# Fused Flamingo layers on one core: the 16-head attention's query projection in split operands, and POOL making all split parts in the layer-1 attention

## The reference

```python
q = (hidden_states @ Wq).reshape(B, Sq, H, D)
k = (encoder_hidden_states @ Wk).reshape(B, Skv, H, D)
v = (encoder_hidden_states @ Wv).reshape(B, Skv, H, D)
q = rmsnorm(q, gq)
k = rmsnorm(k, gk)
scores = jnp.einsum('bqhd,bkhd->bhqk', q, k) * scale
attn = jax.nn.softmax(scores, axis=-1)
out = jnp.einsum('bhqk,bkhd->bqhd', attn, v)
return out.reshape(B, Sq, H * D) @ Wo
```

## Time and profile before

| what | value |
|---|---|
| three runs | 3634.16, 3641.05, 3655.15 us (median 3641.05) |
| the profiled execution's own time | 3635.72 us |
| its span in the trace | 3633.9 us |
| mean granted PE clock | 0.944 of full speed |
| `l0_ffn` | about 245 to 458 us of the span |
| `l1_xattn` | about 458 to 1112 us, main part from about 641 |
| `l2_xattn` | about 1502 to 2920 us |

### The profile page before, as it was taken

The page is one execution under the profiler, slowest core; times in us unless marked ns, Lnnn a source line. Parts: engine busy times, 40 slices in busy tenths (PEclk is TensorE's granted clock), DMA queues, the critical chain, the costliest instruction groups (busy, mean ns, idle before and its releaser), DMA issues. The chain is left out here.

```text
span 3633.9 us, 43465 instructions
## 1 busy us (share of the span) xinstructions
PE 3207.4 (88%) x14597; PEld 1930.8 (53%) x14628; DVE 2598.7 (72%) x3488; ACT 1806.3 (50%) x3413; POOL 1401.9 (39%) x956
## 2 busy tenths in 40 slices
PE   6868888999996888799999999999999878997995
PEld 2337644333333555455555555555555456785763
DVE  6864679877765888377777877777777755665786
ACT  4644333666663445355555556556655332664220
POOL 1121178000000000166666667766666634223540
PEclk9978999999998999899999999999999888998998
DMA  3026736222218100244544454445454345665311
GB/s 127 37 110 228 265 120 164 59 57 58 62 29 175 29 1 1 82 163 152 176 151 158 161 165 167 157 152 167 154 165 136 104 190 200 239 250 189 139 70 58
DMA packets 229735, 478.69 MB, mean 132 GB/s; under 512 B 36224, under 2 KB 69632, under 8 KB 213649
## 3 DMA queue, kind: packets, MB, share of 16 engines
q1 hardware_dynamic: 223280, 459.19, 39.2%
q0 software_dynamic: 6240, 16.81, 1.3%
HBM read 387.51 MB, written 92.06 MB: 132 GB/s over the span
## 5 line engine op out<-in xcount | busy, mean ns | idle before, releaser
L2341 POOL TENSOR_TENSOR l2x_inflow<-l2x_dtu,l2x_rows_b 128x512 f32<-128x512 f32 x256 | 432.3, 1689 | 332.7 <-DVE l2x_state L2230 311.0
L178 POOL TENSOR_TENSOR ln_work<-ln_work,minus_half 128x4 f32<-128x4 f32 (+1 forms) x34 | 33.3, 978 | 1055.4 <-DVE ln_work L166 1055.3
L2230 DVE TENSOR_TENSOR_SCAN l2x_state<-l2x_decay,l2x_inflow 128x512 f32<-128x512 f32 x256 | 384.6, 1502 | 17.0 <-ACT l2x_decay L2104 17.0
L1300 DVE TENSOR_REDUCE l1x_mx<-psum 128x2 f32<-128x1024 f32 x256 | 308.2, 1219 | 96.0 <-PE psum L1142 94.5
L2044 ACT ACTIVATE l2x_probs<-psum,l2x_soft,l2x_norms 128x512 f32<-128x512 f32 x256 | 195.7, 775 | 321.3 <-DVE l2x_soft L2168 321.3
L2357 POOL TENSOR_TENSOR l2x_y_sum<-l2x_y_sum,l2x_state 128x512 f32<-128x512 f32 x224 | 340.6, 1521 | 33.0 <-DVE l2x_state L2239 33.0
L1257 ACT ACTIVATE l1x_split<-psum 128x1024 f32<-128x1024 f32 x256 | 262.2, 1025 | 154.5 <-PE psum L1142 154.5
L126 PE MATMUL psum<-l2x_probs_t,l2x_v_tok 128*128 128x512 f32 x512 | 238.5, 609 | 32.0 <-ACT l2x_probs_t L212 26.0
L2239 DVE TENSOR_TENSOR l2x_state<-l2x_state,l2x_rows_c 128x512 f32<-128x512 f32 x256 | 251.8, 984 | 6.7 <-issue 0.3
L126 PE MATMUL psum<-l2x_xt,l2x_wq 128*128 128x512 f32 x512 | 230.9, 595 | 7.8 <-issue 6.3
L126 PE MATMUL psum<-l2x_kt,l2x_qt 128*128 128x512 f32 x512 | 231.3, 595 | 4.0 <-ACT l2x_probs L2044 4.0
(11 more groups left out here) (446 smaller groups left out, 7311.6 us busy)
## 6 DMA issues: line engine op xcount, KB each, us to landing
l2x_rows_b<-l3x_xd_dram SPq DMA_DIRECT2D x256, 256.0 KB, 3.6
l2x_rows_c<-l3x_xd_dram SPq DMA_DIRECT2D x256, 256.0 KB, 3.5
l2w_raw<-l_w SPq DMA_DIRECT2D x38, 1024.0 KB, 6.3
l2x_wkv<-l2x_kv_dram SPq DMA_DIRECT2D x32, 1024.0 KB, 7.0
l2w_raw<-l_w SPq DMA_DIRECT2D x38, 512.0 KB, 4.6
l1x_heads_dram<-l1x_stage SPq DMA_DIRECT2D x32, 512.0 KB, 3.3
l2x_wq<-l_wq SPq DMA_DIRECT2D x16, 1024.0 KB, 7.2
l2x_wo<-l_wo SPq DMA_DIRECT2D x16, 1024.0 KB, 5.4
```

The source lines that it names most:

```text
L1300: main.drain(dve.tensor_reduce(mx[:, gg % 2, :, j, t], g["psum"][:, b:b + 2, :], AX.X, ALU.max), f"m{n}_0", banks=2)
L2230: dve.tensor_tensor_scan(state[:, s % KEPT, :], decay[:, s % 3, :], inflow[:, s % 3, :], 0.0, ALU.mult, ALU.add).then_inc(scan_done, 1)
L2341: pool.tensor_tensor(inflow[:, s % 3, :], dtu[:], rows_b[:, s % 3, :], ALU.mult).then_inc(inflow_ready, 1)
```

## The change

1. `l0_ffn` no longer makes split parts: the 12 loads, 12 ACT roundings, 12 POOL subtractions and 12 stores go.
2. `l1_xattn` makes them in its main part, with `SPLITS` = 20 pieces: the same 12 and 8 more of two heads of `l2_wq` each. SP loads, and stores 1 MB, in the loop over groups; POOL does both steps (a multiplication by one into float32r, and the subtraction). They use `stage`, for which SP first waits until all heads have been stored.
3. `l2_xattn` projects queries by `split_product` from `q_dram`. The weight is streamed by head, 512 KB each, two buffers. `xt` has two parts: ACT rounds all four chunks, DVE subtracts.
4. To make room: `k_sq` goes (the keys' squares are written into `q_sq`), `KEPT` is 6, `y_sum` has one buffer, so POOL's first addition of a unit waits for DVE's `skip_term` of the unit before.

```diff
@@ l0_ffn
-            def split_load(p):
...
-            def split_store(p):
...
-            def split_round(p):
...
-                act.activation(s_parts[:, 0], s_raw[:, p % 2], ACT.Copy).then_inc(s_hi, 1)
...
             for i in range(NB):
                 if i == 2:
                     scales()
-                split_rest(3 * i)
-                split_rest(3 * i + 1)
                 ln.pool(pool, i)
-                split_rest(3 * i + 2)
@@ l1_xattn, SP
+            def split_load(p):
+                k, b = divmod(p, 4)
+                if p >= SPLITS:
+                    return
+                if p < 12:
+                    src = a[("ctx_t", "l2_wk", "l2_wv")[k]].rearrange("(c p) n -> p c n", p=P)[:, :, b * S:(b + 1) * S]
+                else:
+                    src = a["l2_wq"][2 * (p - 12):2 * (p - 11)].rearrange("h p n -> p h n")
+                if p >= 2:
+                    sp.wait_ge(s_lo, p - 1)
+                sp.dma_start(s_raw[:, p % 2].rearrange("p (c n) -> p c n", c=2), src).then_inc(s_in[p % 2], 16)
+
+            def split_store(p):
...
+                sp.wait_ge(s_lo, p + 1)
...
+            for m in range(2):
+                for k in range(2):
+                    sp.wait_ge(staged_out[m][k], TILES // 2 * 16)
             for gg in range(GROUPS):
                 load_rows(gg)
                 if gg >= 1 and gg + SETS - 1 < GROUPS:
                     load_set(gg + SETS - 1)
+                if gg == 0:
+                    split_load(0)
+                if gg >= 1:
+                    split_store(gg - 1)
+                split_load(gg + 1)
+            sp.wait_ge(s_stored, SPLITS * 16)
@@ l1_xattn, POOL, behind the additions of the bias
+            one = g["ones"][:, 0:1].to_broadcast([P, 2 * S])
+            for p in range(SPLITS):
+                pool.wait_ge(s_in[p % 2], (p // 2 + 1) * 16)
+                if p:
+                    pool.wait_ge(s_stored, p * 16)
+                pool.tensor_tensor(s_parts[:, 0].bitcast(F32R), s_raw[:, p % 2], one, ALU.mult).then_inc(s_hi, 1)
+                pool.wait_ge(s_hi, p + 1)
+                pool.tensor_tensor(s_parts[:, 1].bitcast(F32R), s_raw[:, p % 2], s_parts[:, 0], ALU.subtract
+                                   ).then_inc(s_lo, 1)
             ln.pool(pool, NB - 1)
@@ l2_xattn
-KEPT = 8
+KEPT = 6
...
-            jobs += [(f"xt{(u + 1) // G2}_{c}", "act" if c % 2 else "dve") for c in range(DC)]
+            jobs += [(f"xt{(u + 1) // G2}_{c}", "dve") for c in range(DC)]
...
+            def query_weight(u, h):
+                if u < NU:
+                    if u or h >= 2:
+                        ring.wait_filled(sp, 0, f"q{u}_{h - 2}" if h >= 2 else f"q{u - 1}_{h + 2}")
+                    sp.dma_start(wq[:, h % 2].rearrange("p r c n -> p (r c n)").bitcast(F32),
+                                 g["q_dram"][u % G2 * 4 + h].rearrange("p r n -> p (r n)")).then_inc(wq_in[h % 2], 16)
...
-            weight(wq, "l2_wq", 0, wq_in)
+            query_weight(0, 0)
+            query_weight(0, 1)
...
             weight(wo, "l2_wo", 0, wo_in, rows=True)
-            ring.wait_filled(sp, 0, "q0_3")
-            weight(wq, "l2_wq", 1, wq_in)
+            for h in (2, 3):
+                query_weight(0, h)
+            for h in (0, 1):
+                query_weight(1, h)
...
-                    if n == 15 and u + 2 < NU:
-                        ring.wait_filled(sp, 0, f"q{u + 1}_3")
-                        weight(wq, "l2_wq", u + 2, wq_in)
+                    if n in (7, 8) and u + 1 < NU:
+                        query_weight(u + 1, n - 5)
+                    if n in (11, 13) and u + 2 < NU:
+                        query_weight(u + 2, (n - 11) // 2)
...
-                    ring.fill(product(pe, bank(f"q{u}_{h}"), [(wq[:, c, h * P:(h + 1) * P], xt[:, c, :])
-                                                              for c in range(DC)]))
+                    ring.fill(split_product(pe, bank(f"q{u}_{h}"), [
+                        ([wq[:, h % 2, k, c, :] for k in range(2)], [xt[:, k, c, :] for k in range(2)])
+                        for c in range(DC)]))
...
-                    for c in (1, 3):
+                    if u:
+                        ring.wait_filled(act, 0, f"q{u - 1}_3")
+                    for c in range(DC):
                         job = f"xt{u // G2}_{c}"
                         ring.wait_filled(act, 0, job)
-                        copy(act, "act", ring, job, xt[:, c, :], bank(job))
+                        act.activation(xt[:, 0, c, :], bank(job), ACT.Copy).then_inc(x_hi, 1)
...
+                        dve.wait_ge(x_hi, u // G2 * DC + c + 1)
+                        ring.drain(dve.tensor_tensor(xt[:, 1, c, :], bank(job), xt[:, 0, c, :].bitcast(F32),
+                                                     ALU.subtract), job)
...
                 if n == 1:
-                    since(pool, y_read, u - 1)
+                    since(pool, y_read, u)
```

More of the change, by code:

```diff
@@ L1015, in l1_xattn @@
         staged_out = [[sem(f"staged_out_{n}{k}") for k in range(2)] for n in "qk"]
+        s_hi, s_lo, s_stored = sem("s_hi"), sem("s_lo"), sem("s_stored")
+        s_in = [sem(f"s_in{k}") for k in range(2)]
         set_in = [sem(f"set_in{k}") for k in range(SETS)]
@@ L1371 @@
 GROUPS = NB * NG
+SPLITS = 20
 N_MAX = GROUPS * PAIRS * ST
@@ L1834, in l2_xattn @@
         b_in, c_in = [[sem(f"{n}_in{k}") for k in range(3)] for n in "bc"]
+        wq_in = [sem(f"wq_in{k}") for k in range(2)]
         ln = LayerNorm(g, sem)
@@ L2064, in context @@
                 if u < NU:
+                    if n == "k" and u:
+                        ring.wait_filled(act, 0, f"ssq{u - 1}")
                     for t in range(ST):
```

75 lines of the change are left out of this document (28 added, 47 removed).

## The result

The changed kernel took 3664.55 us (median of eight executions, 3639.33 to 3685.21) against 3641.16 us for the kernel before on the same chip: a ratio of 1.0071, 95% interval 1.005 to 1.0092. That is slower by 23 us, just over what a measurement can tell, and just outside the predicted range. The profiled execution is the slowest of the eight, 3685.21 us, 49.5 us above the profiled one of before.

| stage | before, us | after, us | difference | forecast |
|---|---|---|---|---|
| `l0_ffn` | 196.5 | 192.6 | -3.9 | -5 |
| layer-1 attention | 644.2 | 696.3 | +52.1 | +8 |
| 16-head attention | 1403.7 | 1401.0 | -2.7 | -14.5 |

What follows compares the result with a forecast made beforehand. PE, busy 88% of the span, was taken as the bound. The terms -14.5 (16-head attention), -5 (`l0_ffn`) and +8 (layer-1 attention) made -11.5 us: 3624 us for a profiled execution, 3630 for a median, range 3600 to 3662.

Steps and rivals of the forecast that it cites:

- stall = (4.1 - 3.4)/2 = 0.35: Layer-1 attention, SP's queue: maxima land 4.1 us after issue against 3.4 in reserve; +8 us, bounds 0 and 44.
- The clock rival: 16-head attention: slow PE clock after value 0's longer wait costs 1.7 us in each of 15 units; 3655 us, chance 0.12.
- the three signs of being wrong: Layer-1 waits over 1 us; value 0's wait unchanged at 1.65 us with units 2.6 us shorter; half clock after that wait.
- The rival of SP's queue: Layer-1 attention: the maxima's rows wait behind 1.5 MB at the slow rate, costing 44 us; 3666 us, chance 0.14.
- The reason given for the queue: Layer-1 attention: maxima issued on SP's queue behind a piece's store and load land late, as small transfers do not overtake.
- the bound of 2 us: Layer-1 attention: POOL's pieces blocking DVE's tiny instructions at a group's end; nothing expected, at most +2 us a group.
- the 96 us that one could fear: Layer-1 attention: DVE locked out by POOL's 40 instructions of 2.4 us, by the shared port rule alone; not expected.
- went as forecast: `l0_ffn`: without POOL's subtractions DVE is 2.1 us earlier in the last two batches; -5 us, bounds 0 and -8.
- A unit is shorter by 1.3 us, as forecast: 16-head attention: only queries 2 and 3 give their saving, 1.30 us a unit, -19.5 us over 15 units.
- the copies of `xt`: 16-head attention: ACT makes four copies instead of two, 1.0 us more in each of three batches; +3 us.
- The start: Start of the 16-head attention: the third weight comes 3 to 4 us late, against 2.6 us saved; +2 us (0 to 5).
- No other rival: Remaining rivals, 16-head attention: all of the PE gain arrives, 3602 us, chance 0.23; new product no faster, 3649 us, 0.03.

Runs made afterwards that it cites:

- pool_only: The changed kernel with POOL's splitting work in 16 groups without its loads and stores, only four pieces made with their DMAs (other output); 3620.20 us, ratio 0.9958.
- spaced_decay: The changed kernel with pieces' stores and loads in 18 groups only, and ACT's decays of steps 5 and 6 behind head 0's turned probabilities; 3677.21 us, ratio 1.0134.
- four_pieces: The changed kernel with 4 pieces of splitting instead of 20 in the layer-1 attention (other output); 3637.46 us, ratio 0.9982 to the kernel before.
- dma_only: The changed kernel with all 20 loads and stores of the pieces, but POOL working only on the last four (other output); 3674.32 us, ratio 1.0101.
- pool_wait: The changed kernel with POOL beginning each piece only when the next group's maxima are turned; 3688.37 us, ratio 1.0134 to the kernel before.

## Why the prediction was wrong

**The layer-1 attention is the step that failed**, in the size of one term: "stall = (4.1 - 3.4)/2 = 0.35, taken as 0.4 us in 20 groups, +8 us". The place was right, and so was why PE waits: the maxima land 2.2 to 5.9 us after their issue, and PE waits for their rows. Even the sum of the waits was near, 7.5 us in the first profile (5.5 for rows, the rest behind DVE), 10 and 14 in the other two. What failed is the price and the shape. They are not 0.4 us in twenty groups but 1.3 to 2.2 us in four to eight. And I priced a wait at its own length. The clock rival had the price of a half clock, but I put it into the 16-head attention alone, at 1.7 us a time; in the layer-1 attention show groups of 12.26 us at whole clock, and I never asked what a wait would do there. The term measured +52 us in the first profile, and 44 of them are half clock. Two of the three signs of being wrong that I had named came: waits of over 1 us for the rows, and half clock behind value 0's wait. The rival of SP's queue came out at 3666 us, near the 3664.55 measured, by a sum of waits (44 us) that no profile shows. Its number was right by luck.

**The reason given for the queue was half right.** The Trainium skill's rule (DMA: Bandwidth & Descriptors, "Queues, rings and completion order") that descriptors of one ring are consumed in ring order fits the landing of 5.9 us at 785.03. But with the pieces on another queue, where the maxima were held up less often, the rows of some groups were later still, 6.62 us of wait. So large transfers in flight can hold up a small one of another queue as well. That run also changed when the pieces go out and which engine issues them, so it does not price the two reasons.

**The engines of this layer.** "Only the three tiny instructions at a group's end can be blocked; a piece would have to run there": one did, piece 0, and the bound of 2 us was its price (1.96 against 0.17 us, and a wait of 2.06 us). That "it starts when the store of the one before has landed" leaves out the piece that has none before. PSUM reductions stayed at 1219 ns in the mean, before and after: the rest of POOL's work is free, which pool_only shows. The Trainium skill's rule (SBUF — State Buffer, "SBUF: two separate sides") that the loser of the shared port blocks for a whole instruction agrees with the one collision in SBUF; the 96 us that one could fear by it did not come.

**`l0_ffn`** went as forecast: DVE's instruction takes 0.17 us, PE's two waits for the residuals are 1.1 us each instead of 3.20, and the layer is 3.9 us shorter (5 forecast). Over all profiles it is 194 us in the mean of twelve without the splitting in it and 199 in five with it.

**The 16-head attention.** The windows of one unit without any half clock, before and then after:

```profile
1981.50:2068.20 86.70, 84.47 (x316) 49.03 (x315) 69.36 (x88) 49.48 (x130) 56.87 (x37) 1.00 0.49 153
```

```profile
2035.60:2121.00 85.40, 82.12 (x332) 52.00 (x331) 67.84 (x89) 49.44 (x130) 57.29 (x37) 1.00 0.50 167
```

A unit is shorter by 1.3 us, as forecast: PE has 2.35 us less work and only 1.3 arrives, as the first two queries lie in the half that ACT sets. Value 0 waits 2.29 us in 12 of the 15 units and 0.8 us in three; before, it waited 1.65 us in 11, and not in every unit as the prediction says. The 15 together:

```profile
PE psum L126 <- ACT l2x_probs_t L212: 30.0, 15, 2.3
```

But 15 units took 1285.2 us instead of 1290.1, a gain of 4.9 and not 19.5. The windows give the clock of the 15 units as 0.98 before and 0.97 after. Counted one by one, the stretches at half clock add up to 51 us before and 85 us after. Eight of the new ones, of 3.4 us each, begin right behind value 0's wait of 2.29 us, where before none did. 14.6 us are missing; up to 3 of them can be the copies of `xt`, as forecast, and the rest goes with 34 us more of half clock, 0.34 to 0.43 us each. So the clock rival came true in part here as well, at some 1 us a unit instead of 1.7. The start cost 3.5 us (2 forecast): the third query waited 3.76 us for its weight. In the other profiles the stage lies between 1387 and 1398 us with the split queries (1418 in `spaced_decay`), and between 1397 and 1405 us with the old ones. The means, `spaced_decay` left out, are 1394 us in twelve profiles and 1401.5 in four: the stage gains 7.5 us, half of the forecast. The query product's row has 213.4 us busy and not 180: my 180 were spacings, and busy times overlap (before, the row had 230.9).

The sum against the profiled execution: -4 (`l0_ffn`), +52 and -3, and some 4 us in the other layers: 49.5 us. For the median of the runs it is less, as that execution drew three long stretches. There the change is +23 us; with -5 for `l0_ffn` and -7.5 for the 16-head attention, both by the means of the profiles, some +36 us are left for the layer-1 attention, where the forecast had +8. This last is a difference, and no profile of a median execution shows it. No other rival fits: the new product is faster than the old (12 records from 1882.76 to the next operation at 1885.64 in the after timeline, 2.9 us, 2.79 forecast), and value 0's wait did not stay at 1.65 us.

**What stays open**: why the clock falls behind one wait of 2 us and not behind the next, why it falls 10.8 us behind the first group's wait in five profiles and not in five others, and what sets the length of a stretch.

## What to carry to other kernels

A stage in which PE is busy at 97% with small products has a second price for every wait: here waits of 1.3 to 2.2 us had 10 to 92 us at half clock at them in half of the cases, those of 2.3 us and over in all of them, and each us of it lost 0.33 to 0.43 us. Before large transfers are moved into such a stage, look for the small transfer that PE waits for once per step, and count the time from its issue to its use; an idle engine and idle DMA share say nothing about it. When a kernel's own times spread by 1%, look at the granted clock per stage before explaining a difference.

## What the runs showed of the hardware

I had not expected that half clock lasts so long while PE is fully busy: 54.50 of 54.50 us in four_pieces, 81.44 of 81.70 in dma_only. In the 16-head attention the stretches right behind value 0's wait of 2.29 us last 3.4 us. The number of these stretches differs from one execution to the next, and with it the time of one and the same kernel (three profiles of the changed one: 3644 to 3685 us, with 1 to 3 long ones). A 16 KB store took 1.4 us in most groups without a piece and up to 6.0 us with 1.5 MB in flight (`pool_wait`). Putting those 1.5 MB on a queue of their own gave fewer late stores, but longer waits for the 4 KB loads (6.62 us). And a DVE instruction on 16 columns in SBUF took 1.96 us beside POOL's work on SBUF, while DVE's reductions from PSUM took their usual time.
